# One order for every unit on TensorE, and a timetable with at most one piece per unit

## What is computed

```
x = x + 0.5 * ffn(layernorm(x))
# state-space layer on h = layernorm(x) * norm_w + norm_b, and h @ Win -> x_ssm, z  (512 channels each)
x_ssm = silu(causal depthwise convolution of x_ssm, 4 taps, + conv_b)
dt = softplus(x_ssm @ dt_w + dt_b);  A = -exp(A_log)          # 512 channels x 64 states
Bt = x_ssm @ Bp;  Ct = x_ssm @ Cp
state[d,s] = state[d,s] * exp(dt[d] * A[d,s]) + dt[d] * x_ssm[d] * Bt[s]    # over 512 tokens
y[d] = sum_s state[d,s] * Ct[s] + D[d] * x_ssm[d]
x = x + (x + (y * silu(z)) @ Wout)     # norm of x in front; both residuals are kept
x = x + 0.5 * ffn(layernorm(x))
```

## Time and profile before

| | |
|---|---|
| median of 3 runs | 5445.08 us (5436.83 to 5452.04) |
| profiled execution | 5417.77 us, span of the core 5415.9 us |
| PE / DVE / ACT / POOL busy | 90% / 90% / 72% / 93% of the span |
| granted TensorE clock, mean | 0.988 of full speed; below full speed in the first slices only |
| scans on DVE | 4096, mean 1199 ns; first at 187 us |
| products with C on POOL | 2048, mean 2386 ns |
| chain that ended last | PE 32%, POOL 32%, DVE 22% |

### The profile page before, as it was taken

How to read it: one execution, slowest core, us unless ns; L and a number is a source line. 1 busy time by engine, 2 the same in 40 slices (tenths; PEclk the granted TensorE clock), 3 DMA queues, 4 the chain that set the end, 5 groups by cost and what they waited for, 6 DMA issues and landing times.

```text
span 5415.9 us, 189369 instructions
## 1 busy us (share of the span) xinstructions
PE 4892.5 (90%) x85070; PEld 2799.0 (52%) x85070; DVE 4877.0 (90%) x4595; ACT 3903.5 (72%) x6659; POOL 5017.8 (93%) x2310
## 2 busy tenths in 40 slices
PE   4698999989999999999999999998999999999887
PEld 2354555555555555555555555555555555555554
DVE  1599999999999999999998999999999998999996
ACT  3777787777778777787777778677787777766564
POOL 0599999999999999999998999999999999999997
PEclk8899999999999999999999999999999999999999
DMA  5475565656556565665656656565565756556553
GB/s 170 145 178 188 172 190 186 176 192 173 188 181 182 191 175 197 174 187 190 176 190 167 194 181 179 193 178 189 179 184 183 179 192 174 187 180 173 194 184 118
DMA packets 578860, 976.04 MB, mean 180 GB/s; under 512 B 294881, under 2 KB 328450, under 8 KB 510466
## 3 DMA queue, kind: packets, MB, share of 16 engines
q1 hardware_dynamic: 313858, 961.82, 54.9%
q10 hardware_dynamic: 264192, 2.11, 3.0%
HBM read 875.74 MB, written 88.08 MB: 178 GB/s over the span
## 4 chain that ended last, share of the span: by engine, by line
PE 32%; POOL 32%; DVE 22%; issue 9%; DMA 3%; ACT 1%; SPq 0%; ACTq 0%; DVEq 0%; POOLq 0%
POOL H L661 29%; DVE H L603 19%; PE pUB L724 11%; PE Y L748 9%; PE pP L682 4%; PE pP L688 4%; DMA Bd<-scratch_diag 3%; PE pA L779 2%; DVE cv L554 2%; PE pA L773 2%; POOL duo L648 1%; POOL dto L642 1%; POOL lnv L637 1%; DVE X L558 0%; PE Y L737 0%
## 5 line engine op out<-in xcount | busy, mean ns | idle before, releaser
L661 POOL TENSOR_TENSOR H<-H,Cb 128x1024 f32<-128x1024 f32 x2048 | 4783.7, 2386 | 202.5 <-DVE H L603 198.4
L603 DVE TENSOR_TENSOR_SCAN H<-dA,pUB 128x512 f32<-128x512 f32 x4096 | 4634.1, 1199 | 344.6 <-PE pUB L724 329.1
L440 ACT ACTIVATE dA<-DT,w_negA 128x512 f32<-128x512 f32 x4096 | 2619.4, 710 | 1324.3 <-DVE H L603 1320.6
L724 PEld LDWEIGHTS pUB<-Bd,UT 64*64 64x64 f32 x65536 | 1868.6, 133 | 1884.3 <-DVE H L603 1051.3
L724 PE MATMUL pUB<-Bd,UT 64*64 64x128 f32 x65536 | 2234.2, 273 | 398.2 <-DVE H L603 312.1
L748 PE MATMUL Y<-H,w_ident 64*64 64x512 f32 x16384 | 2169.9, 598 | 5.9 <-POOL H L661 5.3
L748 PEld LDWEIGHTS Y<-H,w_ident 64*64 64x64 f32 x16384 | 516.4, 133 | 302.3 <-issue 245.6
L682 PE MATMUL pP<-hT,w_Win 128*128 128x512 f32 x512 | 263.9, 639 | 15.3 <-DVE cv L554 12.1
L688 PE MATMUL pP<-U,w_dt_w 128*128 128x512 f32 x512 | 260.2, 633 | 6.6 <-DVE absv L617 4.8
L440 ACT ACT_TABLE_LOAD x178 | 228.4, 1283 | 3.2
L554 DVE SCALAR_TENSOR_TENSOR cv<-pP,w_conv_w,cv 128x511 f32<-128x511 f32 (+2 forms) x192 | 139.2, 725 | 32.3 <-ACT cv L378 32.1
(11 more groups left out here) (80 smaller groups left out, 1701.0 us busy)
## 6 DMA issues: line engine op xcount, KB each, us to landing
Cb<-scratch_c SPq DMA_DIRECT2D x512, 1024.0 KB, 5.2
Bd<-scratch_diag SPq DMA_DIRECT2D x512, 512.0 KB, 6.0
scratch_diag<-H SPq DMA_DIRECT2D x16, 1024.0 KB, 16.9
scratch_z<-zo SPq DMA_DIRECT2D x64, 256.0 KB, 5.9
scratch_dt<-dto SPq DMA_DIRECT2D x64, 256.0 KB, 8.2
scratch_ut<-uto SPq DMA_DIRECT2D x64, 256.0 KB, 7.5
DT<-scratch_dt SPq DMA_DIRECT2D x64, 256.0 KB, 5.3
UT<-scratch_ut SPq DMA_DIRECT2D x64, 256.0 KB, 5.8
```

Source lines behind the costliest of these rows:

```text
L440: last = nc.scalar.activation(dA[:, n % DAR, j, :], DT[:, k, :], ACT.Exp, scale=c["negA"][:, k, GS * blk + j:GS * blk + j + 1])
L603: last = nc.vector.tensor_tensor_scan(H[:, u % HR, 2 * i + j, :], dA[:, n % DAR, 2 * i + j, :], pUB[:, i, :].rearrange("p (t s) -> p s t", ...
L661: nc.gpsimd.tensor_tensor(h[:, j:j + 2, :], h[:, j:j + 2, :], Cb[:, blk % 2, j:j + 2, :], ALU.mult).then_inc(times_c, 1)
L724: last = nc.tensor.matmul(out, UT[rows, k, j * P + h * HP:j * P + h * HP + HP], Bd[rows, blk % 2, i, j * P:(j + 1) * P].rearrange("p (t s) ...
```

## The change

PE's order becomes the same for each unit: block (n+1, 0), piece, block (n+1, 1), half a sum. `add_states` handles a half (two states) in one go, with the same wait on POOL; it is executed behind the second block, where before its first quarter stood ahead of it.

```
-                    if n % 2:
-                        other(b, n, close, proj, ffn)
-                    sum_states(b, n, 0, scan, close)
+                    other(b, n, close, proj, ffn)
                     if scan and n + 1 < GN:
                         force(b, n + 1, 1)
                     if proj and n + 1 == GN:
                         force(b + 1, 0, 1)
-                    if n % 2 == 0:
-                        other(b, n, close, proj, ffn)
-                    sum_states(b, n, 1, scan, close)
+                    sum_states(b, n, scan, close)
...
-            def add_states(b, n, j):
-
-                if j % 2 == 0:
-                    pe.wait_ge(times_c, at(2 * (GN * b + n + 1) + j // 2 + 1))
+            def add_states(b, n, half):
+
+                pe.wait_ge(times_c, at(2 * (GN * b + n + 1) + half + 1))
+                for j in (2 * half, 2 * half + 1):
...
+            def sum_states(b, n, scan, close):
+
+                p, half = (n - 4, 1) if n % 2 == 0 else (n - 3, 0)
```

All six tables get new numbers. Of them, PE's and the first of ACT's:

```
-PES = {"xs": (0, 4, 8, 12), "z": (3, 7, 11, 15), "BC": ((18, 19),), "turn b": (22,), "dt": ((24, 25), (30, 31), (36, 37), (42, 43)),
+PES = {"xs": (0, 4, 8, 12), "z": (2, 6, 10, 14), "BC": ((16, 18),), "turn b": (19,), "dt": ((20, 22), (26, 28), (32, 34), (38, 40)),
-LATER = {"y": ((5, 6), (9, 10)), "ffn 1": ((20, 21), (26, 27)), "ffn c": ((38, 39), (44, 45))}
+LATER = {"y": ((5, 9), (13, 17)), "ffn 1": ((25, 27), (29, 33)), "ffn c": ((41, 42), (44, 45))}
-ACTS = {"tap": (2, 6, 10, 14), "u": (5, 9, 13, 17), "z": (5, 9, 13, 17), "BC": (21,), "B": (24,),
+ACTS = {"tap": (1, 5, 9, 13), "u": (3, 7, 11, 15), "z": (3, 7, 11, 15), "BC": (19,), "B": (20,),
```

More of the change, by code:

```diff
@@ L739, in skip_over @@
                 last.then_inc(skip, 1)
[L741 to L762 removed]
+            def add_states(b, n, half):
+                pe.wait_ge(times_c, at(2 * (GN * b + n + 1) + half + 1))
+                for j in (2 * half, 2 * half + 1):
+                    for r in range(2):
+                        rows = slice(r * HP, r * HP + HP)
+                        for i in range(2):
+                            last = nc.tensor.matmul(Y[r][i * HP:i * HP + HP, :], c["ident"][rows, rows], H[rows, (GN * b + n + i) % HR, j, :],
+                                                    start=False, stop=(n % HALF == HALF - 2 and j == GS - 1))
+                if half:
+                    last.then_inc(summed, 2)
             def transpose(i, done):
@@ L852, in other @@
                         transpose(i, t2)
+            def sum_states(b, n, scan, close):
+                p, half = (n - 4, 1) if n % 2 == 0 else (n - 3, 0)
+                if scan and p >= 0:
+                    if p % HALF == 0 and half == 0:
+                        skip_over(b, p)
+                        skip_over(b, p + 1)
+                    add_states(b, p, half)
+                if close and p < 0:
+                    add_states(b - 1, GN + p, half)
             def step(b, scan, close, proj, ffn):
```

27 lines of the change are left out of this document (6 added, 21 removed), and 6 rows, old and new, of the table ACTS.

## The result

The changed kernel takes **5633.56 us** (median of 4 runs, 5627.57 to 5639.92); the kernel before, run beside it, 5443.74. The ratio is **1.0349**, 95% interval 1.0333 to 1.0365. The forecast was 5458 with a range of 5365 to 5520: the time lies 114 us above the range. Slower held the largest chance, but at 5458 to 5495 us, 0.2 to 0.9% (rival (e), with 5758, was given 0.01).

A forecast was written before the change was run, and what follows sets the result against it. DVE's own work plus its waits was taken to set the step, unchanged at 325.5 us. Profiled 5417.8 + 15 (start) - 1 (last step) = 5432, plus the median's offset: 5458 us, range 5365 to 5520.

The forecast's parts named there:

- (e): Rival: a drain behind each table load on ACT, 20 us a step, giving 5758 us; chance 0.01.
- What bounds the kernel, and the unit lengths: DVE's own work plus its waits set the step, POOL's 314 us is the floor behind; a unit takes 4.44 us.
- What the change does to PE: Isolated large piece makes DVE wait 0.6 us, before 0.7 to 0.8; pairs are won; block behind large piece costs 0.1 more.
- the walk: Unit-by-unit sum of one step with DVE's, PE's and ACT's waits: 323.6 us, 325.5 with handoffs and late blocks.
- What the change does to ACT: ACT waits for PE's products with DVE's decays behind: 0.8 us for z three times a step, up to 1.8 for dt.
- The waits that were worked out: DVE's waits on ACT within a step, behind z's projections and the logarithms, 0.3 to 2.3 us each.
- The sum over a step: 325.5 us against 325.45 before, so no gain, with 3 us of error on 50 terms.
- The start: Ahead of the first scan, feed-forward pieces at dt products add 5.7 us and norms 10.0: about +15, bounds 0 and +20.
- (a): Rival: ACT's waits fall from 10 to about 5 us a step, step 320.7, time 5386 us; chance 0.28.
- (b): Rival: a PE block behind a 128-wide piece costs 0.3 us more, 2.5 us a step, time 5495; chance 0.22.
- (c): Rival: nearly all waits go and the step stops at POOL's 314 us, time 5293; chance 0.03.
- (d): Rival: the timetable costs nothing ahead of the first scan, step as forecast, time 5444 us; chance 0.04.

The follow-up runs named there:

- e_ubuf: Changed kernel, but ACT copies u0 into an idle tile in unit 62 and the term of D reads that copy, so the silu needn't wait: 5456.1 us, ratio 1.0077.
- e_order: PE's new order with all six tables of the kernel before: 5407.3 us, ratio 0.9981 to the kernel before.
- e_u4: Changed kernel with u0 and z0 moved from ACT's unit 3 to unit 4: 5559.3 us, ratio 1.0267 to the kernel before.
- e_skip: Changed kernel with the term of D put ahead of PE's second block in slots 3 and 35: 5558.1 us, ratio 1.0264 to the kernel before.

## Why the prediction was wrong

**What bounds the kernel, and the unit lengths: right.** Step less DVE's waits is 304.4 to 305.6 us in every kernel here. That the two add up to the step is bookkeeping; what the runs show is that DVE's work stays the same, and that POOL was idle for 8 us of a step or more in each of them, so it never became the floor.

**What the change does to PE: right, except for sizes.** DVE's waits for PE fell from 20.6 to 6.4 us per step in e_ubuf (102 us in 16 steps), where the profile was to show 150 to 200 us in all. Some lie hidden under the waits for ACT: in e_order they are 14.6. The prediction also misread the pair of unit 6 and 7: between its give-back and its projection the order shows one quarter and one block, not two quarters. A block behind a large piece costs nothing more (1.91 against 1.92), where I took 0.1. Half a sum is 1.71 to 1.72 from start to start in the new order, where the walk had 1.75.

**What the change does to ACT: this is the step that failed.** It listed ACT's waits for what it *reads*: z's product, dt's product. It left out a wait for what it *overwrites*. The sentence "three times a step (the fourth hides behind the gates)" looked at z0 in unit 3, and passed over u0 in front of it in the same unit, which waits for `skip`. The gates were what made it late, and not what hid it: gates, scans, second block, term of D, silu, z, table load, decays. The prediction had this wait at nothing. Its price, 9.26 us in front of unit 4 and 1.51 at the first tap of unit 5, against 0.17 there in e_ubuf, is 10.6 us of the 14 that the step is longer than the 325.5 of the walk; e_ubuf, without it, has a step shorter by 11.9. e_ubuf, e_u4 and e_skip show it from three sides. The semaphore could be seen before: `act.wait_ge(skip, ...)` stands in `silu_u`, and the order shows `skip_over` going behind the block.

**The waits that were worked out came as worked out.** z at 8, 12 and 16: forecast 0.8, 0.7 and 0.8, measured 1.11, 0.58 and 1.11. The logarithms: forecast 2.3 and 0.3 at 25 and 24, 1.2 at 31, 1.7 at 43; measured 2.17, 0.38, 1.68 and 1.65. Two small ones were missed: norm 2's last passes in front of 48 (2.43) and norm 3's in front of 56 (1.04), both ACT waiting for POOL's step of a norm (L212), which comes with POOL's lag.

**The sum over a step: 325.5, and without the missed wait 327.7.** An error of 2.2 us on 50 terms, inside the 3 that the prediction allowed. A part of that is luck: the two small waits alone are 3.5 us, and terms that came out smaller, those of PE among them, made up for some of it.

**The start: +15 forecast, +8.9 measured, in one traced execution of each kernel.** It isn't sharper than some 3 us: up to the first scan e_skip executes what the kernel after does, and its first scan came at 198.6 against 195.9, with a granted clock of 0.79 against 0.80. The chain of norm 2 and 3 behind the last logarithm in ACT's timeline of the kernel after:

```profile
168.97 0.58 ACT L411 ACTIVATE pP<-absv 128x512 f32<-128x512 f32 x1
...
183.91 2.07 ACT L219 ACTIVATE XN<-XA,norms 128x256 f32<-128x256 f32 x4 [0.61 <-POOL norms L212]
```

From the end of the last logarithm (169.55) to the end of the last normalization (185.98) it is 16.4 us; the earlier trace rows have 5.7 us from 170.84, where the last logarithm ended, to 176.58. That is +10.7, forecast +10.0. The mis-sized term is the other one: the logarithm ends 1.3 us earlier than before (169.55 against 170.84), where I had the dt products 5.7 us later for the feed-forward pieces between them. So those pieces didn't lengthen the chain.

**The rivals.** (a) ACT's waits half as large: wrong, they were whole. (b) block behind a piece: wrong. (c) POOL at 314: never reached. (d) start free: wrong, it was 8.9 us. (e) drain at a table switch: wrong again; 1922.72 and 1.28 end at 1924.00, and the decays begin at 1924.02. The Trainium skill, page "ScalarE: Activation LUTs", section "What ACT_TABLE_LOAD costs", has that drain; no row of these kernels shows it. The true case was none of the five, and no list of other sizes for the same waits could have found it. A list of the waits of each moved instruction would have.

## What to carry to other kernels

When a change moves an instruction in an in-order engine, write down all of its semaphore waits, also those that guard the buffer that it overwrites, and for each what now stands ahead of the releasing instruction on *its* engine. An instruction moved earlier and its releaser moved later meet in a place that neither edit shows alone: here each half moved by one or two slots, and 10 us a step lay between them.

Where a wait is removed and the time doesn't follow, look at the queue that only issues transfers. Here a load behind a wait for the slowest engine, with unrelated transfers between, was worth 0.8% and 0.6%, when three and two entries of its table were moved; and a store moved by two slots made a wait of its own. Look at the granted clock in the same place too: some of what seemed to be waits that moved were steps at the lower clock.
